# Layer norms between stages: gate products on GpSimd with interleaved centering, and two consecutive norms made in one pass

## What is computed

```python
def _layernorm(x, axis=-1, eps=1e-05):
    m = jnp.mean(x, axis=axis, keepdims=True)
    v = jnp.var(x, axis=axis, keepdims=True)
    return (x - m) / jnp.sqrt(v + eps)

xn = _layernorm(x)
s = _L2_attn_ref(xn, ...)
g = _silu(_L2_ffn_ref(xn, ...))      # starts with x1 = layernorm(xn, ln1_g, ln1_b)
x = x + s * g
xn = _layernorm(x)
s = _L3_attn_ref(xn, ...)            # starts with layernorm(xn, ln_g, ln_b)
```

## Time and profile before

| what | us |
|---|---|
| median of 3 runs | 4407.21 |
| lowest and highest run | 4401.78, 4411.33 |
| the profiled execution | 4403.99 |
| its span, first to last instruction | 4402.1 |
| TensorE busy in the span | 3562.2 (81%) |
| VectorE busy | 2629.4 (60%) |
| ScalarE busy | 2108.2 (48%) |
| GpSimd busy | 1698.5 (39%) |

### The profile page before, as it was taken

How to read it: one execution, slowest core, us unless ns; L and a number is a source line. 1 busy time by engine, 2 the same in 40 slices (tenths; PEclk the granted TensorE clock), 3 DMA queues, 4 the chain that set the end, 5 groups by cost and what they waited for, 6 DMA issues and landing times. The chain is left out here.

```text
span 4402.1 us, 79023 instructions
## 1 busy us (share of the span) xinstructions
PE 3562.2 (81%) x26972; PEld 2564.8 (58%) x26972; DVE 2629.4 (60%) x6366; ACT 2108.2 (48%) x5657; POOL 1698.5 (39%) x1896
## 2 busy tenths in 40 slices
PE   5888807656999978999996888884999999995581
PEld 2555603433666645666664888772777777774461
DVE  3666672433666645666664666663788888885233
ACT  4666604333665643544444444444666666661120
POOL 3554540303666643333330000000666666672505
PEclk7999958877999998999998999997999999996795
DMA  3777620012000000000001000001222222223122
GB/s 110 205 197 184 174 91 0 9 33 45 1 1 1 2 6 6 2 1 2 1 2 39 0 0 0 0 0 35 66 76 76 76 76 73 76 78 107 57 69 63
DMA packets 232672, 224.58 MB, mean 51 GB/s; under 512 B 59209, under 2 KB 176905, under 8 KB 232074
## 3 DMA queue, kind: packets, MB, share of 16 engines
q1 hardware_dynamic: 225642, 206.52, 16.9%
q0 software_dynamic: 4096, 8.40, 0.6%
q10 hardware_dynamic: 2592, 5.26, 0.3%
HBM read 166.10 MB, written 54.00 MB: 50 GB/s over the span
## 5 line engine op out<-in xcount | busy, mean ns | idle before, releaser
L2159 DVE TENSOR_TENSOR_SCAN a_h<-a_dA,a_dBu_psum 128x512 f32<-128x512 f32 x512 | 595.9, 1205 | 164.5 <-issue 105.0
L1160 POOL TENSOR_SCALAR a_probs<-a_probs,a_row_inv 128x128 f32<-128x128 f32 (+1 forms) x512 | 381.3, 762 | 324.0 <-DVE a_row_inv L1146 324.0
L2116 POOL TENSOR_TENSOR a_h<-a_h,main_g 128x512 f32<-128x512 f32 x256 | 385.1, 1506 | 270.4 <-DVE a_h L2159 260.3
L1658 DVE SCALAR_TENSOR_TENSOR m_acc<-m_o_psum,m_gate,m_acc 128x128 f32<-128x128 f32 x992 | 297.8, 346 | 116.9 <-PE m_o_psum L1622 116.5
L1883 PE MATMUL a_dBu_psum<-a_B_diag,a_dt_u_turned 64*128 64x128 f32 x4096 | 317.0, 289 | 21.6 <-DVE a_h L2159 20.8
L1622 PEld LDWEIGHTS m_o_psum<-m_values,m_hidden 128*128 128x128 f32 x2048 | 313.9, 197 | 30.0 <-ACT m_hidden L1640 2.6
L1614 PE MATMUL m_h_psum<-m_x,m_keys 128*128 128x256 f32 x1024 | 327.8, 411 | 0.0
L1640 ACT ACTIVATE m_hidden<-m_h_psum 128x256 f32<-128x256 f32 x512 | 196.2, 383 | 265.0 <-PE m_h_psum L1614 265.0
L1622 PE MATMUL m_o_psum<-m_values,m_hidden 128*128 128x128 f32 x2048 | 314.5, 280 | 0.0
L1485 POOL TENSOR_TENSOR r_position_q<-r_turned_q 128x512 f32<-128x512 f32 x128 | 159.9, 1271 | 388.9 <-DVE r_turned_q L1530 388.9
L1442 ACT ACTIVATE r_probs<-r_logits_psum,r_neg_max 128x256 f32<-128x256 f32 x512 | 235.1, 475 | 140.4 <-DVE r_neg_max L1536 140.4
(11 more groups left out here) (540 smaller groups left out, 8244.4 us busy)
## 6 DMA issues: line engine op xcount, KB each, us to landing
main_g<-a_b_c_rows SPq DMA_DIRECT2D x256, 256.0 KB, 3.1
a_band_rows<-main_g SPq DMA_DIRECT2D x64, 512.0 KB, 3.4
a_B<-a_band_rows SPq DMA_DIRECT2D x192, 128.0 KB, 3.2
a_A<-a_band_rows SPq DMA_DIRECT2D x192, 128.0 KB, 3.1
f_x_rows<-f_zero ACTq DMA_DIRECT2D x16, 320.0 KB, 9.3
f_x_expert<-f_x_rows SPq DMA_DIRECT2D x16, 320.0 KB, 2.8
f_y_rows<-f_y_expert SPq DMA_DIRECT2D x16, 320.0 KB, 2.2
f0b_stage_w<-L_ffn_up_weights SPq DMA_DIRECT2D x9, 512.0 KB, 4.3
```

The source lines that it names most:

```text
L1160: ins = nc.gpsimd.tensor_scalar(pr[:, h % NPR, tile[t]], pr[:, h % NPR, tile[t]], rinv[:, p % NST, q:q + 1], None, ALU.mult)
L1658: ins = nc.vector.scalar_tensor_tensor(out=acc[:, t, :], in0=o, scalar=gate[:, t, e:e + 1], in1=acc[:, t, :], op0=ALU.mult, op1=ALU.add)
L2116: tt(h[:, r, :, :], h[:, r, :, :], Cs[:, g % NCS, :, :], ALU.mult).then_inc(hc_pool, 1)
L2159: nc.vector.tensor_tensor_scan(flat, dA[:, M % NDA, q, k, :, :].rearrange("p n t -> p (n t)"), db[:, 2 * (g % 2) + k, :], 0.0, ALU.mult, A ...
```

## The change

The norm helper is written anew and two of its calls go:
- With gate and norm, GpSimd makes the products g * s of all eight units; without a norm (the last call) it makes those of the odd units and VectorE those of the even ones. VectorE centers unit k - 1 right behind the sum of unit k.
- On TensorE and ScalarE variance and Ln come two units behind (LAG = 2) and not one.
- The scale and shift of unit k - 1 comes behind the product of unit k.
- With `again`, the norm makes a second output: the norm of its own output with scale and shift. The mean of the normed data is zero and its variance var / (var + eps), so the second factor is (var (1 + eps) + eps^2) to the power -1/2: a second Ln and a second Exp for each unit on ScalarE, and on VectorE an operation that multiplies by gamma and this factor, and one that adds beta. The vectors come by DMAs in the same call (`loads`). The call after layer 1 makes the input of the relative attention so, in g, and the one after layer 2 that of the scan stage, in s.
- The call at L1671 with its load, the call at L1705 and two of the 20 loads of `l3_attention` are taken out. The relative attention reads its input from g and writes its output to g.

```diff
@@ -73,7 +73,7 @@
     c = {
-        "earlier": scope.sb("earlier", [P, P]), "eps": scope.sb("eps", [P, 1]),
+        "earlier": scope.sb("earlier", [P, P]), "eps": scope.sb("eps", [P, 1]), "eps_twice": scope.sb("eps_twice", [P, 1]),
     }
@@ -83,6 +83,7 @@
                 nc.gpsimd.memset(c["eps"][:], LN_EPS)
+                nc.gpsimd.memset(c["eps_twice"][:], LN_EPS * LN_EPS)
                 nc.gpsimd.memset(c["ident"][:], 0.0)
                 nc.gpsimd.memset(c["earlier"][:], 1.0).then_inc(filled, 1)
                 pool.wait_ge(filled, 1)
@@ -113,99 +114,157 @@
-def gate_and_norm(nc, c, x, xn, s=None, g=None, gate=False, norm=True, out=None, affine=None):
+def gate_and_norm(nc, c, x, xn, s=None, g=None, gate=False, norm=True, out=None, affine=None, again=None, loads=()):
     W = BANK
     N = x.shape[1] // W
-    NBUF, NPS = 3, 4
+    NBUF, NPS, LAG = 3, 4, 2
     with Scope(nc, "norm") as q:
         if norm:
             sq = q.sb("squares", [P, NBUF, W])
             rs = q.sb("inv_dev", [P, N, W])
             mean = q.banks("mean", NPS)
             var = q.banks("var", NPS)
-        gated, mixed, x_new, mean_ready, centered, squared, var_ready, logged, rooted, normed, stored = q.sems(
-            "gated mixed x_new mean_ready centered squared var_ready logged rooted normed stored")
+        if again is not None:
+            rs2 = q.sb("inv_dev_twice", [P, N, W])
+        (gated, mixed_pool, mixed_dve, x_new, mean_ready, centered, squared, var_ready, logged, rooted, normed, twice, stored,
+         landed) = q.sems("gated mixed_pool mixed_dve x_new mean_ready centered squared var_ready logged rooted normed twice "
+                          "stored landed")
         def cols(k):
             return slice(k * W, (k + 1) * W)
+        def on_pool(k):
+            return norm or k % 2 == 1
+        def before(k):
+            return sum(1 for i in range(k + 1) if on_pool(i) == on_pool(k))
         with nc.Block() as block:
             @block.scalar
             def _(act):
+                def square(k):
+                    act.wait_ge(centered, k + 1)
+                    if k >= NBUF:
+                        act.wait_ge(var_ready, k - NBUF + 1)
+                    nc.scalar.activation(sq[:, k % NBUF, :], xn[:, cols(k)], ACT.Square).then_inc(squared, 1)
+                def take_log(k):
+                    act.wait_ge(var_ready, k + 1)
+                    ins = nc.scalar.activation(rs[:, k, :], var[:, k % NPS, :], ACT.Ln, bias=c["eps"][:])
+                    if again is not None:
+                        ins = nc.scalar.activation(rs2[:, k, :], var[:, k % NPS, :], ACT.Ln, bias=c["eps_twice"][:],
+                                                   scale=1.0 + LN_EPS)
+                    ins.then_inc(logged, 1)
+                def root(k):
+                    act.wait_ge(logged, k + 1)
+                    ins = nc.scalar.activation(rs[:, k, :], rs[:, k, :], ACT.Exp, scale=-0.5)
+                    if again is not None:
+                        ins = nc.scalar.activation(rs2[:, k, :], rs2[:, k, :], ACT.Exp, scale=-0.5)
+                    ins.then_inc(rooted, 1)
                 if gate:
                     for k in range(N):
                         nc.scalar.activation(g[:, cols(k)], g[:, cols(k)], ACT.Silu).then_inc(gated, 1)
                 if norm:
-                    def take_log(k):
-                        act.wait_ge(var_ready, k + 1)
-                        nc.scalar.activation(rs[:, k, :], var[:, k % NPS, :], ACT.Ln, bias=c["eps"][:]).then_inc(logged, 1)
+                    for k in range(N + LAG):
+                        if k < N:
+                            square(k)
+                        if k >= LAG:
+                            take_log(k - LAG)
+                    for k in range(N):
+                        root(k)
+            if gate:
+                @block.gpsimd
+                def _(pool):
+                    for k in range(N):
+                        if on_pool(k):
+                            pool.wait_ge(gated, k + 1)
+                            nc.gpsimd.tensor_tensor(g[:, cols(k)], g[:, cols(k)], s[:, cols(k)], ALU.mult).then_inc(mixed_pool, 1)
+            @block.vector
+            def _(dve):
+                def product(k):
+                    dve.wait_ge(gated, k + 1)
+                    nc.vector.tensor_tensor(g[:, cols(k)], g[:, cols(k)], s[:, cols(k)], ALU.mult).then_inc(mixed_dve, 1)
+                def add(k):
+                    dve.wait_ge(mixed_pool if on_pool(k) else mixed_dve, before(k))
+                    nc.vector.tensor_tensor(x[:, cols(k)], x[:, cols(k)], g[:, cols(k)], ALU.add).then_inc(x_new, 1)
+                def center(k):
+                    if gate:
+                        dve.wait_ge(x_new, k + 1)
+                    dve.wait_ge(mean_ready, k + 1)
+                    nc.vector.tensor_tensor(xn[:, cols(k)], x[:, cols(k)], mean[:, k % NPS, :],
+                                            ALU.subtract).then_inc(centered, 1)
+                def scale(k):
+                    dve.wait_ge(rooted, k + 1)
+                    if again is not None:
+                        nc.vector.scalar_tensor_tensor(out=again[0][:, cols(k)], in0=xn[:, cols(k)], scalar=again[1],
+                                                       in1=rs2[:, k, :], op0=ALU.mult, op1=ALU.mult).then_inc(twice, 1)
+                    nc.vector.tensor_tensor(xn[:, cols(k)], xn[:, cols(k)], rs[:, k, :], ALU.mult).then_inc(normed, 1)
+                def shift(k):
+                    if affine is not None:
+                        dve.wait_ge(normed, k + 1)
+                        nc.vector.tensor_scalar(xn[:, cols(k)], xn[:, cols(k)], affine[0], affine[1], ALU.mult, ALU.add)
+                    if again is not None:
+                        dve.wait_ge(twice, k + 1)
+                        nc.vector.tensor_scalar(again[0][:, cols(k)], again[0][:, cols(k)], again[2], None, ALU.add)
+                for k in range(N + 1):
+                    if gate and k < N:
+                        if not on_pool(k):
+                            product(k)
+                        add(k)
+                    if norm and k >= 1:
+                        center(k - 1)
+                if norm:
+                    if loads:
+                        dve.wait_ge(landed, 16 * len(loads))
                     for k in range(N + 1):
                         if k < N:
-                            act.wait_ge(centered, k + 1)
-                            if k >= NBUF:
-                                act.wait_ge(var_ready, k - NBUF + 1)
-                            nc.scalar.activation(sq[:, k % NBUF, :], xn[:, cols(k)], ACT.Square).then_inc(squared, 1)
+                            scale(k)
                         if k >= 1:
-                            take_log(k - 1)
-                    for k in range(N):
-                        act.wait_ge(logged, k + 1)
-                        nc.scalar.activation(rs[:, k, :], rs[:, k, :], ACT.Exp, scale=-0.5).then_inc(rooted, 1)
-            @block.vector
-            def _(dve):
-                if gate:
-                    for k in range(N):
-                        dve.wait_ge(gated, k + 1)
-                        nc.vector.tensor_tensor(g[:, cols(k)], g[:, cols(k)], s[:, cols(k)], ALU.mult).then_inc(mixed, 1)
-                        dve.wait_ge(mixed, k + 1)
-                        nc.vector.tensor_tensor(x[:, cols(k)], x[:, cols(k)], g[:, cols(k)], ALU.add).then_inc(x_new, 1)
-                if norm:
-                    for k in range(N):
-                        if gate:
-                            dve.wait_ge(x_new, k + 1)
-                        dve.wait_ge(mean_ready, k + 1)
-                        nc.vector.tensor_tensor(xn[:, cols(k)], x[:, cols(k)], mean[:, k % NPS, :],
-                                                ALU.subtract).then_inc(centered, 1)
-                    for k in range(N):
-                        dve.wait_ge(rooted, k + 1)
-                        nc.vector.tensor_tensor(xn[:, cols(k)], xn[:, cols(k)], rs[:, k, :], ALU.mult).then_inc(normed, 1)
-                        if affine is not None:
-                            dve.wait_ge(normed, k + 1)
-                            nc.vector.tensor_scalar(xn[:, cols(k)], xn[:, cols(k)], affine[0], affine[1], ALU.mult,
-                                                    ALU.add)
+                            shift(k - 1)
             if norm:
                 @block.tensor
                 def _(pe):
+                    def average(k):
+                        if gate:
+                            pe.wait_ge(x_new, k + 1)
+                        if k >= NPS:
+                            pe.wait_ge(centered, k - NPS + 1)
+                        nc.tensor.matmul(mean[:, k % NPS, :], c["mean"][:], x[:, cols(k)], start=True,
+                                         stop=True).then_inc(mean_ready, 1)
                     def variance(k):
```

(46 more changed lines are left out.)

## The result

| | us |
|---|---|
| changed kernel, median of 4 runs | 4339.44 (4335.16 to 4341.14) |
| kernel before, beside it, median of 4 runs | 4404.49 (4396.62 to 4411.33) |
| ratio | 0.9851, 95% interval 0.9832 to 0.9870 |
| the profiled execution of after, and its span | 4335.16, 4333.4 |

The change saves 1.5%, 65 us between the medians and 68.7 between the two spans. The forecast was 4339.8, with 67.4 saved. It came out so closely in part by luck: the median from which it was counted, 4407.2, sank to 4404.5 with the fourth run, and terms that were off made up for each other, as the stages show. I cut both traces at the barriers. Each stretch runs from the first thing that it does to that of the next one: a DMA, the table load ahead of silu in the gated norms (in the last gate silu itself), the first mean matmul in the last norm of layer 2, the first activation in the scan.

What follows compares the result with a forecast made beforehand. The prediction took the kernel as a chain of stages with all-engine barriers, so savings add up: 34.6 + 31.3 + 7.6 - 7.8 + 2.5 + 1.2 - 2.0 = 67.4 off 4407.2 gives 4339.8 us, range 4326 to 4354.

Steps and rivals of the forecast that it cites:

- parts 1 and 2: Second norm of layer 2 with its load, and norm of layer 3 with two DMAs, go: 34.6 and 31.3 us less.
- The vector DMAs at the head of the gated norms: Six DMAs on SyncE's queue, needed only ahead of the scaling over 20 us later: cost nothing if landed by then.
- That GpSimd and VectorE exclude each other: In gated norms and last gate, GpSimd's SBUF reads and VectorE's two-SBUF-input operations block each other; first mean 1.75 us later.
- The rival without exclusion: Gated norms and last gate: engines do not block each other, last gate gains 2.4; 4331.7 us, chance 0.18.
- the slow relative attention: Relative attention runs at TensorE's low clock; if half of it did, +330, 4670 us; chance 0.02.
- Part 3: Gated norm after layer 0: shorter body with products on GpSimd, Exp pass 7.6 us sooner.
- a third from T + 3.6 and a fourth, done by T + 5.8 if the clock rises at T + 4.5: Gated norm's early TensorE matmuls, T being the first mean's start; last variance then starts at T + 15.3.
- the second rival: Gated norms: TensorE's clock stays low, last variance 11.9 us later in the plain one; total 4372 us, chance 0.05.
- its sign, matmuls 1.70 apart beyond the first four: Listed as showing the forecast wrong: TensorE matmuls still 1.70 us apart after the first four.
- Part 4: Two norms with a second output: Exp pass 5.2 us sooner, tail 9.2 longer, net loss 3.9 each, 7.8 for two.
- Part 5: Plain norms that stay: gain 2.5 us in layer 2's norm, 1.2 in the kernel's first norm.
- Part 6: Last gate: products split between GpSimd and VectorE, 12.7 us and not 10.7, a loss of 2.0.

Runs made afterwards that it cites:

- experiment 1: Changed kernel with all gate products back on VectorE: ratio 0.9831 to the kernel before; norm after layer 0 29.4 us.
- experiment 3: Changed kernel's new norm body in all calls, but the two second norms kept as calls with their loads: ratio 0.9939 to the kernel before.
- experiment 7: Changed kernel with eight idle-filling 128-column matmuls ahead of each norm's first mean: ratio 0.9853 to the kernel before.
- experiment 8: Changed kernel with gate products on VectorE and the second output's Ln, Exp and two-operation product left out: ratio 0.9784, median 4310.65 us.
- experiment 9: Kernel before with three unused tiles, so later tiles lie where the changed kernel has them: ratio 1.0001, attention of layer 2 644.0 us.
- 10: Changed kernel with products on VectorE, no second factor, and eight extra matmuls ahead of each norm's first mean: ratio 0.9801 to the kernel before.
- experiment 6: Changed kernel run again unchanged: ratio 0.9835 to the kernel before, relative attention 703.0 us.

## Why the prediction was right, and where it was not

**Steps that held.** The removed passes (parts 1 and 2): 34.6 and 31.4 against 34.6 and 31.3, read off the starts on both sides, since barriers let nothing hide. The vector DMAs at the head of the gated norms cost nothing. That GpSimd and VectorE exclude each other held in both directions: GpSimd's product at a median of 1.71, sums of up to 1.76, and 8.4 us less when one engine does it all (experiment 1). The Trainium skill, "SBUF — State Buffer", in the text on the engine ports, says the same of the shared port pair; the trace agrees, the sum of two SBUF tiles stood for up to 1.07 us longer than alone, while the centering, with one input in PSUM, kept its 0.69. The rival without exclusion, 4331.7, is out: its gain in the last gate was to be 2.4, and there was a loss of 1.2. So is the slow relative attention, 4670: the stage took 706.0 and 703.0, before it 702.6 and 704.2.

**Part 3, the gated norm after layer 0: 5.1 and not 7.6.** The step that failed is "a third from T + 3.6 and a fourth, done by T + 5.8 if the clock rises at T + 4.5". It failed in two places. The smaller: VectorE's order is sum 1, centering 0, sum 2, and the centering waits for the first mean; then the third sum (738.09) stands for GpSimd, 1.73 and not 0.69, so the third mean comes at T + 4.6. I had left the centering between the sums out. The larger: TensorE stays at its low pace to T + 9.4. Experiment 3 gives each its price, as two of its calls have the same late third mean and the full pace from it on. Their first Exp comes at T + 19.0, 0.5 later than the 18.5 worked out; here it comes at T + 21.1, another 2.1 later. This is the mechanism of the second rival (low clock, as the stream starts with waits), which I had priced at all or nothing, 11.9; its sign, matmuls 1.70 apart beyond the first four, is in the trace. What decides the pace is not shown. The third mean is late in every one of the nine gated calls of experiment 3 and the two traces of the changed kernel; five of them, the three after layer 0 among them, stay low to T + 8 or later, and four are fast from that mean on. After layers 1 and 2 the same code was fast in one trace and slow in the next.

**Part 4, the double norms: +5.0 and +5.8 and not +3.9.** Timelines of the norm after layer 1, after: TensorE, ScalarE, VectorE.

```profile
921.71 3.66 PE L242 MATMUL norm_mean_psum<-main_x,main_mean 128*128 128x512 f32 x4 [7.07 <-DVE main_x L195]
...
930.47 0.69 ACT L155 ACTIVATE norm_inv_dev<-norm_var_psum,main_eps 128x512 f32<-128x512 f32 x1
931.06 0.68 ACT L157 ACTIVATE norm_inv_dev_twice<-norm_var_psum,main_eps_twice 128x512 f32<-128x512 f32 x1
931.63 0.63 ACT L151 ACTIVATE norm_squares<-main_xn 128x512 f32<-128x512 f32 x1
...
943.73 0.63 ACT L163 ACTIVATE norm_inv_dev<-norm_inv_dev 128x512 f32<-128x512 f32 x1
...
926.74 1.16 DVE L195 TENSOR_TENSOR main_x<-main_x,main_g 128x512 f32<-128x512 f32 x1
927.82 0.67 DVE L201 TENSOR_TENSOR main_xn<-main_x,norm_mean_psum 128x512 f32<-128x512 f32 x1
...
946.25 0.75 DVE L207 SCALAR_TENSOR_TENSOR main_g<-main_xn,main_vectors_l,norm_inv_dev_twice 128x512 f32<-128x512 f32 x1
946.91 0.69 DVE L209 TENSOR_TENSOR main_xn<-main_xn,norm_inv_dev 128x512 f32<-128x512 f32 x1
947.51 0.48 DVE L217 TENSOR_SCALAR main_g<-main_g,main_vectors_l 128x512 f32<-128x512 f32 x1
947.91 0.75 DVE L207 SCALAR_TENSOR_TENSOR main_g<-main_xn,main_vectors_l,norm_inv_dev_twice 128x512 f32<-128x512 f32 x1
```

The tail is right: 15.4 us from the first Exp (943.73) to the next stage's DMA (959.09), against 6.3 before, 9.1 longer and 9.2 worked out. A unit takes 1.66 (946.25 to 947.91, worked out 1.68), the two-operation product 0.66 of it and the addition 0.40, where I had 0.61 and 0.46. The head was mis-sized. The first Ln comes at T + 8.8, not T + 8.1: I had the third centering wait for its mean alone, but on VectorE it stands behind the fourth sum (926.74), which takes 1.16 beside GpSimd's product, and starts at T + 6.1 (927.82). And an Ln is followed by the next activation after 0.57, not 0.54 (931.06 to 931.63), 12.0 for the 21 activations and not 11.3. So the Exp pass starts at T + 22.0, not 20.8. After layer 2, where TensorE stayed at its low pace as after layer 0, the first Ln comes at T + 9.4 and the Exp pass at T + 23.0. From the first Ln on ScalarE runs 21 activations almost without a gap, which is why TensorE's pace is worth only 0.7 to 1.1 here (experiment 7) and experiment 8 gives much.

**Part 5** held: 2.7 and 1.3 against 2.5 and 1.2. TensorE in the last norm of layer 2 after:

```profile
2308.58 2.81 PE L242 MATMUL norm_mean_psum<-main_g,main_mean 128*128 128x512 f32 x6 [1.30 <-PEq L52]
...
2319.81 2.74 PE L249 MATMUL norm_var_psum<-norm_squares,main_mean 128*128 128x512 f32 x6
```

Before, the last variance started 14.55 after the first mean (rows 10); now it is the third of three from 2319.81, 2319.81 + 2 x 0.86 - 2308.58 = 12.95, against 12.9 worked out. The scalar pass gave the other 1.0. But here too the pace at the start differs between executions: the kernel before took 28.7 in one and 30.0 in the next, the changed one 26.0 in both, and 27.5 to 27.7 in three variants with the same code in this call.

**Part 6, the last gate: +1.2 and not +2.0.** VectorE, then GpSimd, after:

```profile
4318.60 0.69 DVE L191 TENSOR_TENSOR main_g<-main_g,main_s 128x512 f32<-128x512 f32 x1 [3.26 <-ACT main_g L169]
4319.32 3.35 DVE L195 TENSOR_TENSOR main_x<-main_x,main_g 128x512 f32<-128x512 f32 x2
4322.59 1.75 DVE L191 TENSOR_TENSOR main_g<-main_g,main_s 128x512 f32<-128x512 f32 x1
4324.37 2.23 DVE L195 TENSOR_TENSOR main_x<-main_x,main_g 128x512 f32<-128x512 f32 x2
...
4319.17 6.29 POOL L185 TENSOR_TENSOR main_g<-main_g,main_s 128x512 f32<-128x512 f32 x4 [7.36 <-ACT main_g L169]
```

The exclusion is there (two sums 3.35, a product 1.75), and GpSimd's four products take 6.29 in one row. What was too dear is its price: from the first product to the end of the last sum 11.9 us (4318.60 to 4330.46) against 12.7. I had added each operation of VectorE at its full 0.61 to GpSimd's time; a product beside a sum takes 1.71 in the median, 0.45 more than the 1.26 alone, so part of each operation lies outside the exclusion. How much of the 0.8 this makes I did not resolve.

**What made the total meet.** 4.3 us missing in the norms were made up by 5.6 in stages that I had set to zero. Of these, some 3 us in the attention of layer 2 go with the tiles' new places, and perhaps 1.4 in the scan (experiment 9). The rest differs from execution to execution: layer 0 ran at 687 to 702 us over all traces, whatever the kernel, and the relative attention at 703 to 707 (without the eight matmuls of experiments 7 and 10), where the 3.4 here lie in its first 59 us (experiment 6). And the base moved: between the medians 65 us were saved and not 67.4. The forecast's point was good to 0.4 us, its terms to 4.

## What to carry to other kernels

Where every stage ends in a barrier, a dropped pass can be read off the starts on both sides and is worth all of it. To hand part of an elementwise step from VectorE to GpSimd can lose: here it cost 8.4 us in four calls, as both read two SBUF tiles at once. Look in the trace for a sum that takes twice its time beside GpSimd, and price every place where the orders cross, not only the first. Where a short stage starts with waits, price a slow start of TensorE as a case of its own, between none and all. And before a second output is made exactly, ask how far it is from the first: a factor within some 1e-5 of one (as long as the variance is not much below one) cost 15 us here.

## What the runs showed of the hardware

- The place of the tiles in SBUF changed a DMA's time: 34.20 us for the store of the bias rows, 33.36 with 4 bytes a partition more allocated ahead of it, 32.50 with 28.
- The pace of TensorE at a stage's start differs between executions of the same code, which is worth 0.9 to 1.7 us in the norms here (after layer 2 43.4 and 42.5 in the two traces of the changed kernel, the last norm of layer 2 26.0 there and 27.7 in experiment 3): the same three means of the last norm of layer 2 took 2.81 in the changed kernel and 4.33 in experiment 1, where that call has the same code:

```profile
2309.29 4.33 PE L242 MATMUL norm_mean_psum<-main_g,main_mean 128*128 128x512 f32 x6 [1.30 <-PEq L52]
```
